# Moving z and the residual sum of x2 between ACT, GpSimd and DVE in an adaLN block with experts

## The chip, the cores and the metric

The kernel runs on one core of a Trainium2 chip. TensorE is called PE here, VectorE DVE, ScalarE ACT, GpSimd POOL and SyncE SP. The metric is the time of one execution on the device in microseconds; times are medians of several runs.

## The reference, cut to what matters

There are 16 batch elements of 512 tokens with 128 channels. For each one the block does attention and then a mixture of experts:

```python
h = layernorm(x) * (1 + ca) + sa
Q, K, V = (h @ W.T).reshape(16 heads, ...)            # 8 channels a head
out = softmax(Q @ K.T) @ V                            # in fp32 accuracy
y = out + h
x = x + ga * (y - mean(y)) / sqrt(var(y) + eps)       # mean and var over all 512 x 128 of the element
h = layernorm(x) * (1 + cb) + sb
logits = h @ gate_w;  top 2 of 8 experts, softmax weights
x = x + gb * weighted sum of the two experts' (silu(h @ w1 + b1) * (h @ w2 + b2)) @ w3 + b3
```

The code calls `z` the value ga * (y - mean) / sqrt(var + eps), with channels on partitions, and `x2` the sum x + z with tokens on partitions. x2 is the input of the second layernorm and, at the end, the residual of the output.

## The kernel before, in words

The attention part is a software pipeline of stages b = 0 to 16, one for each batch element and one more. A stage is 16 quads (r = 0 to 15) of four steps (h = 0 to 3). In step (b, r, h) PE makes a 128 x 512 tile of scores of element b (`pass_a`), DVE takes the negated row maximum of it from PSUM (`maximum`), and, 12 quads later, PE makes the tile again transposed with the maxima subtracted (`pass_b`), ACT takes its exponential (`exps`), and PE multiplies with V (`values`). Three PSUM banks hold the tiles of each pass, so PE is at most three tiles ahead of DVE and of ACT.

Everything else is put into the gaps of this stream, in an order written out by hand for each engine: `side(b, r, h)` on DVE, `stage` on POOL and SP, `before` and `halfway` on ACT, `misc_uses` on PE. Each engine works through its own list in order. One PSUM bank, `misc`, serves all small matmuls and transposes; the next fill of it waits until the one before has been read (`s_misc_read`). Stage b also finishes element b - 2 (its attention output, y, mean, variance, z, x2) and does the second layernorm, the routing and the row scatter of element b - 3.

The names which the steps speak of, in the order of a stage:

- z of element b - 2: ACT's `end_z` in quad 14 (L1822, an activation with scale and bias, which POOL's `y_move` computes as `y_scale` and `y_shift`, L918 and L920), PE's `z_turn` in quad 15, and DVE's `end_x2` (L1376), which reads the turned z in PSUM and adds x (`x_back`), after the last maximum of the stage.
- At the head of the next stage DVE does `front_x2` (`bn_stats` of x2, two tiles in step (0, 0) and two in (0, 2)), `front_sums` (L1253) in (1, 0), `end_inv` (L1299) in (2, 0) and `front_norm2` (L1390) in quad 3.
- POOL at the same time does `split_max` of the stage just ended (it needs all 64 maxima of it), `relay_v` (L900), `f_sums` and `front_power` (L911, L1030: 1/sqrt of the variance), `max_move` (L892, two DMAs), `scatter(b - 4, 1)` (four indirect DMAs, L1099), `front_rows` (L1037, L1044), `add_h` (L1018, L1025: y), `split_q`, `split_k`, `split_max` of the first half, `choose` and what follows it, `y_power`, `y_move`, `x_rows` (L991, L994), `places` (L973, which waits for DVE's `front_pos` in step (13, 3)), `second_score` (L968, which waits for DVE's `first_score` in (14, 1)), `front_slots`, and `scatter(b - 3, 0)`, four indirect DMAs more.
- PE turns `rows` in quad 5 (`h_turn`, L2046), needs `max_rows` in quads 1 and 9, and fills `v` in quad 0.
- ACT copies the normalized rows to the second slot (`row_copy`, L1839) in quad 12.
- After stage 16 an expert phase of 39 blocks follows, into which the last two elements' steps are woven. For these two, x2 is still made on DVE.

SP stores x2 (`x2_store`) and loads the next x (`x_back_load`) at the head of a stage, ahead of the store of `inv` and the loads of the next Q and K.

Of the kernel before, what the change touches and what calls it, by code (L numbers as in the profile page):

```python
# [125 lines left out]
def build(nc, x, wqT, wkT, wvT, w1, b1T, w2, b2T, w3, b3, gate_w, cT, wmod, out):  # L126
    ctx = ExitStack()
    with ctx:
# [255 lines left out]
        s_y_shift = sem("s_y_shift")  # L384
        s_z = sem("s_z")
        s_x2_stored = sem("s_x2_stored")

# [96 lines left out]
        def scattered(eng, n):  # L484

            eng.wait_ge(s_y_scattered[n % Y_RING], (n // Y_RING + 1) * BT * DMA)

        def wait_apart(eng, semaphore, value):
# [21 lines left out]
        def _(sp):  # L510
# [113 lines left out]
            def x_back_load(b):  # L624
                if later(b):
                    wait_apart(sp, s_misc_read, misc_index("z_turn", b - 1) + 1)
                sp.dma_start(x_back[:], x[b].rearrange("(t p) c -> p t c", p=P)).then_inc(s_x_back, DMA)

            def x2_store(b):
                wait_apart(sp, s_misc_read, misc_index("z_turn", b) + 1)  # L630
                sp.dma_start(x2_dram[b].rearrange("(t p) c -> p t c", p=P), x2_out[:]).then_inc(s_x2_stored, DMA)
# [202 lines left out]
        def _(pool):  # L834
# [52 lines left out]
            def max_move(b, side):  # L887

                pool.wait_ge(s_misc_read, misc_index("max_rows", b, side) + 1)
                for a in range(2):  # L890
# [3 lines left out]
                                   max_rows[at:at + PARTS * MCOLS // 2]).then_inc(s_max_moved, DMA)  # L894

            def relay_v(b, par):
                wait_apart(pool, s_v_loaded, (b + 1) * 4 * DMA)
                if later(b, 2):
                    wait_apart(pool, s_pv, (b - 1) * QUADS)
                pool.tensor_copy(Vt[:, par, :, 0:DK], v_land[:]).then_inc(s_v_relaid, 1)  # L900
# [11 lines left out]

            def y_move(b):

# [4 lines left out]
                pool.wait_ge(s_y_scale, b + 1)  # L919
                pool.tensor_tensor(y_shift[:], y_mean[:], y_scale[:], ALU.mult).then_inc(s_y_shift, 1)  # L920

# [160 lines left out]
            def front_slots(f):  # L1082
# [9 lines left out]
                pool.wait_ge(s_w_col, f + 1)  # L1092
                pool.wait_ge(s_h_row, 2 * (f + 1))
                pool.wait_ge(s_token, 2 * (f + 1))

            def scatter(f, k):

                for t in range(TT):
                    pool.indirect_dma_start(rows_dram, bass.IndirectOffsetOnAxis(ap=slot[:, k, t:t + 1], axis=0),  # L1099
                                            rows[:, f % 2, k, t], None).then_inc(s_scattered[f % 2], DMA)  # L1100

            def stage(b, par):
                if has(b, 1, NB):
                    split_max(b - 1, 1)
                if has(b, 0, NB - 1):
                    relay_v(b, par)
                if has(b, 3, NB):
                    f_sums(b - 3)
                    front_power(b - 3)
                if has(b, 1, NB):  # L1110
                    max_move(b - 1, 1)
                if has(b, 4, NB):
# [36 lines left out]
                if has(b, 2, NB - 1):  # L1149
                    y_move(b - 2)  # L1150
                if has(b, 1, NB - 4):
# [51 lines left out]
        def _(dve):  # L1203
# [175 lines left out]
            def front_x2(f, tiles):  # L1379

                dve.wait_ge(s_misc_read, misc_index("z_turn", f) + 1)
                for t in tiles:
# [204 lines left out]
            def side(b, r, h):  # L1587

                if has(b, 3, NB):
                    if r == 0 and h in (0, 2):  # L1590
                        front_x2(b - 3, (h, h + 1))
                    if (r, h) == (1, 0):
                        front_sums(b - 3)
                    if r == 3:
# [7 lines left out]
                if has(b, 2, NB + 1):  # L1602
                    if (r, h) == (2, 0):
                        end_inv(b - 2)
                    if (r, h) == (7, 0) and b == NB:
                        end_stats(b - 2)
# [55 lines left out]
            def stage(b, par):  # L1662
                for r in range(QUADS):
                    for h in range(4):
                        side(b, r, h)
                        if has(b, 0, NB - 1):
                            maximum(b, r, h)
                    if r == 15 and has(b, 2, NB - 1):
                        end_x2(b - 2)

# [101 lines left out]
        def _(act):  # L1772
            act.wait_ge(s_c, DMA)
            act.activation(c_silu[:], c_sb[:], ACT.Silu).then_inc(s_c_silu, 1)
            def evacuate(what, b, g=0):
# [24 lines left out]
                if what == "h_turn":  # L1800
                    if later(b):
                        act.wait_ge(s_misc_full, misc_index("logits", b - 1) + 1)
                    ins = act.activation(h2T[:], misc[:], ACT.Copy)
                ins.then_inc(s_misc_read, 1)

# [11 lines left out]
            def end_z(b):  # L1817

                act.wait_ge(s_y_shift, b + 1 if b < NB - 1 else NB - 1)
                if later(b):  # L1820
                    act.wait_ge(s_misc_full, misc_index("z_turn", b - 1) + 1)
                act.activation(z[:], y[:], ACT.Identity, bias=y_shift[:], scale=y_scale[:]).then_inc(s_z, 1)  # L1822
# [62 lines left out]
            def stage(b, par):  # L1885

                def before(r):
                    if r == 13 and has(b, 1, WCOPY):
                        expert_first(b - 1)
                    if r == 14 and has(b, 2, NB - 1):  # L1890
                        end_z(b - 2)
                    if r == 10 and has(b, 3, NB):
                        front_gap(b - 3)

                def halfway(r):
                    for q, what, ub, g in misc_uses(b):
                        if q == r and what in ("x_turn", "q", "k", "v", "max_rows", "h_turn"):
                            evacuate(what, ub, g)
                    if r == 7 and has(b, 2, NB - 1):
                        y_sum_all(b - 2)  # L1900
                    if r == 10 and has(b, 2, NB - 1):
                        y_squares(b - 2)
                    if r == 12 and has(b, 3, NB):
                        row_copy(b - 3)
# [331 lines left out]
```

## Time and profile before

| | us |
|---|---|
| median of 3 runs | 1076.61 (1074.5 to 1076.93) |
| the profiled execution | 1079.33 |
| its span, first to last instruction | 1077.6 |
| PE, DVE, ACT, POOL busy | 948.9, 899.9, 815.1, 725.5 |

The profile shows one execution. Busy time is the time in which an engine's instructions ran; issuing instructions and waits are not in it. A line of the timeline has the start and the length in microseconds, the engine, the line of the kernel, the operation with its output and inputs, and how many instructions were merged; in brackets stands the idle time ahead of it with the engine and line that ended it. The mean granted clock of PE over the span is 0.966 of its full speed.

### The profile page before, as it was taken

The page shows a single profiled execution, that of the slowest core. Times are in us where ns is not written, and L with a number is a line of the kernel's source. Part 1 is how long each engine was busy: PE and PEld are TensorE (multiplying, and loading weights), DVE is VectorE, ACT ScalarE, POOL GpSimd, SP SyncE. Part 2 cuts the span into 40 slices and gives each one's busy share as a digit, 9 for nine tenths or more (in the row PEclk, how much of TensorE's full clock was granted, in tenths as well). Part 3 has the DMA queues.
Part 4 walks back from the last instruction along what each step waited for, and adds up shares of the span by engine and source line. Part 5 has one row for each costly group of instructions (what it writes and reads, how often), then busy time and mean ns, then how long its engine had stood idle before and what let it go on. Part 6 is the DMA issues. An engine that isn't in the chain of part 4 may idle for free. (4 is left out here: it accounts for less than half of the span.)

```text
span 1077.6 us, 19369 instructions
## 1 busy us (share of the span) xinstructions
PE 948.9 (88%) x5725; PEld 362.9 (34%) x5725; DVE 899.9 (84%) x1891; ACT 815.1 (76%) x1563; POOL 725.5 (67%) x1198
## 2 busy tenths in 40 slices
PE   4699898999999999999999999889798998799970
PEld 2112122222222222222222222222135775577640
DVE  5797999998999999999999999999646767355766
ACT  2127898998889998999989999889676786477630
POOL 4853143877878778787787876665747677777761
PEclk9998999999999999999999999999799999899995
DMA  9859768756668567675676756631334445354546
GB/s 217 138 140 226 140 190 158 150 153 119 180 130 160 143 128 184 130 156 153 124 184 129 160 139 127 165 85 49 90 109 103 149 150 164 118 153 156 174 157 248
DMA packets 367832, 159.68 MB, mean 148 GB/s; under 512 B 289248, under 2 KB 332144, under 8 KB 364016
## 3 DMA queue, kind: packets, MB, share of 16 engines
q1 hardware_dynamic: 347376, 122.06, 50.7%
q0 software_dynamic: 11136, 19.61, 5.5%
q10 hardware_dynamic: 9216, 16.78, 4.5%
q8 instruction: 46, 0.75, 0.3%
q14 instruction: 58, 0.48, 0.2%
HBM read 87.85 MB, written 71.82 MB: 148 GB/s over the span
## 5 line engine op out<-in xcount | busy, mean ns | idle before, releaser
L1292 DVE TENSOR_REDUCE neg_max<-bank 128x1 f32<-128x512 f32 x1024 | 641.5, 681 | 40.5 <-PE bank L2071 35.2
L1848 ACT ACTIVATE probs<-bank 128x512 f32<-128x512 f32 x1024 | 545.7, 610 | 71.4 <-PE bank L2083 69.1
L2071 PE MATMUL bank<-Kt,Qt 48*128 48x512 bf16 x1024 | 336.6, 398 | 41.6 <-DVE neg_max L1292 31.8
L2083 PE MATMUL bank<-Qt,Kt 51*128 51x512 bf16 x1024 | 331.1, 392 | 7.9 <-ACT probs L1848 5.7
L2096 PE MATMUL bank<-probs,Vt 128*16 128x512 f32 x2048 | 275.4, 610 | 0.0
L2071 PEld LDWEIGHTS bank<-Kt,Qt 48*128 48x128 bf16 x1024 | 73.4, 94 | 374.0 <-DVE neg_max L1292 328.1
L1183 POOL DMA_INDIRECT y_dram<-y_rows,row_in x156 | 153.0, 981 | 58.3 <-issue 44.2
L1099 POOL DMA_INDIRECT rows_dram<-rows,slot x128 | 129.3, 1010 | 49.4 <-issue 35.2
L1974 ACT ACTIVATE probs<-bank,w3b_cur 128x512 f32<-128x512 f32 x78 | 53.5, 688 | 57.4 <-PE bank L2121 57.4
L1726 DVE SCALAR_TENSOR_TENSOR probs<-bank,w3b_cur,probs 128x512 f32<-128x512 f32 x78 | 58.3, 749 | 38.9 <-ACT probs L1974 38.2
L2083 PEld LDWEIGHTS bank<-Qt,Kt 51*128 51x128 bf16 x1024 | 74.5, 94 | 42.1 <-ACT probs L1848 34.1
L2187 PE MATMUL bank<-probs,w3b_cur 128*128 128x512 f32 x156 | 73.3, 592 | 0.0
L2119 PE MATMUL bank<-ht_first,w_cur 128*128 128x512 f32 x156 | 69.7, 447 | 1.7 <-DVE probs L1726 1.6
L1659 DVE TENSOR_TENSOR ht_rest<-bank,ht_first 128x512 fp32r<-128x512 f32 x39 | 26.9, 690 | 47.9 <-ACT ht_first L1946 47.7
L2120 PE MATMUL bank<-ht_rest,w_cur 128*128 128x512 f32 x156 | 62.7, 402 | 0.0
L2121 PE MATMUL bank<-ht_first,w_cur 128*128 128x512 f32 x156 | 62.2, 399 | 0.0
L2096 PEld LDWEIGHTS bank<-probs,Vt 128*16 128x16 f32 x2048 | 33.7, 94 | 74.5 <-issue 50.2
L892 POOL DMA_DIRECT2D Qt<-max_rows x64 | 43.9, 687 | 16.8 <-ACT max_rows L1799 15.0
L495 POOL CAST max_parts<-neg_max 128x32 bf16<-128x32 f32 x32 | 8.5, 265 | 55.6 <-DVE neg_max L1292 55.5
L1857 ACT ACTIVATE o_sb<-bank 128x512 f32<-128x512 f32 x64 | 38.5, 602 | 8.6 <-PE bank L2096 8.4
L1957 ACT ACTIVATE w_cur<-w_parts 128x1024 fp32r x37 | 39.1, 1057 | 0.2
L2106 PE MATMUL bank<-ident,row_in 128*128 128x128 f32 x156 | 24.4, 280 | 15.1 <-DMA row_in<-rows_dram 14.9
(254 smaller groups left out, 1237.6 us busy)
## 6 DMA issues: line engine op xcount, KB each, us to landing
o_dram<-o_sb ACTq DMA_DIRECT2D x64, 256.0 KB, 2.7
row_in<-rows_dram SPq DMA_DIRECT2D x39, 260.0 KB, 2.9
Qt<-q_dram SPq DMA_DIRECT2D x64, 128.0 KB
Kt<-k_dram SPq DMA_DIRECT2D x64, 128.0 KB
y_in<-y_dram SPq DMA_DIRECT2D x16, 512.0 KB, 4.6
q_dram<-q_parts SPq DMA_DIRECT2D x48, 128.0 KB, 4.9
k_dram<-k_parts SPq DMA_DIRECT2D x48, 128.0 KB, 5.8
rows_dram<-rows SPq DMA_DIRECT2D x4, 1040.0 KB, 5.3
```

Source lines behind the costliest of these rows:

```text
L1099: pool.indirect_dma_start(rows_dram, bass.IndirectOffsetOnAxis(ap=slot[:, k, t:t + 1], axis=0), rows[:, f % 2, k, t], None).then_inc(s_sca ...
L1183: pool.indirect_dma_start(y2_dram, bass.IndirectOffsetOnAxis(ap=row_in[n % RING][:, t, AT_TOKEN:AT_TOKEN + 1].bitcast(U32), axis=0), y_row ...
L1292: dve.tensor_reduce(neg_max[:, side, a, col:col + 1], score_a[m % 3][:], AX_X, ALU.max, negate=True).then_inc(s_max, 1)
L1726: dve.scalar_tensor_tensor(hidden[n % 2][:, c], up_value[c][:], w3b_cur[n % 3][:, AT_B2 + c:AT_B2 + c + 1], gate_act[c], ALU.add, ALU.mult ...
L1848: act.activation(probs[:, 4 * (j % 2) + (k ^ 1)], score_b[n % 3][:], ACT.Exp).then_inc(s_exp, 1)
L2071: pe.matmul(score_a[m % 3][:], Qt[b % BUFS][first:first + ROWS, n, P * c:P * c + P], Kt[b % BUFS][first:first + ROWS, n], start=True, stop ...
L2083: pe.matmul(score_b[m % 3][:], Kt[b % BUFS][first:first + ROWS + PARTS, n, P * c:P * c + P], Qt[b % BUFS][first:first + ROWS + PARTS, n], ...
L2096: ins = pe.matmul(pv_bank[32 * h:32 * h + 2 * DK, :], Vt[:, par, 4 * (N8 * a + n) + c], probs[:, 4 * (j % 2) + h], start=(c == 0), stop=(c ...
L2119: pe.matmul(to[:], w[:, 0, at], ht_first[n % 2][:], start=True, stop=False)
L2120: pe.matmul(to[:], w[:, 0, at], ht_rest[n % 2][:], start=False, stop=False)
L2121: ins = pe.matmul(to[:], w[:, 1, at], ht_first[n % 2][:], start=False, stop=True)
L2187: ins = pe.matmul(yt_bank[:], w3b_cur[n % 3][:, D * c:D * c + D], hidden[n % 2][:, c], start=(c == 0), stop=(c == HC - 1))
```

## The change

z of elements 0 to 13 is made on POOL by a `tensor_scalar` (`y_center` in place of `y_move`), which adds the negated mean and multiplies by the scale; `end_z` on ACT remains for the last element only. The turned z is copied from PSUM into `x2_out` by ACT, halfway through quad 15, in place of the sum on DVE; POOL adds x in place at the head of the next stage (`x2_add`), behind `split_max` and ahead of `relay_v`, and signals the new semaphore `s_x2`. The readers of x2 (`front_x2`, the store, the next load of x) wait for that. On POOL `max_move` now stands ahead of `f_sums` and `front_power`. On DVE `front_x2` goes from quad 0 to quad 1 and `front_sums` from (1, 0) to (2, 0), behind `end_inv`. `row_copy` goes from quad 12 to quad 15 on ACT, and the scatter of slot 0 no longer waits for it; that of slot 1 does.

```diff
+        def x2_made(eng, b):
+
+            if b < FIRST_LAST:
+                eng.wait_ge(s_x2, b + 1)
+            else:
+                eng.wait_ge(s_misc_read, misc_index("z_turn", b) + 1)
...
             def x_back_load(b):
                 if later(b):
-                    wait_apart(sp, s_misc_read, misc_index("z_turn", b - 1) + 1)
+                    x2_made(sp, b - 1)
...
             def x2_store(b):
-                wait_apart(sp, s_misc_read, misc_index("z_turn", b) + 1)
+                x2_made(sp, b)
...
+            def x2_add(b):
+
+                pool.wait_ge(s_misc_read, misc_index("z_turn", b) + 1)
+                pool.wait_ge(s_x_back, (b + 1) * DMA)
+                pool.tensor_tensor(x2_out[:], x2_out[:], x_back[:], ALU.add).then_inc(s_x2, 1)
...
-            def y_move(b):
+            def y_center(b):
...
-                pool.tensor_tensor(y_shift[:], y_mean[:], y_scale[:], ALU.mult).then_inc(s_y_shift, 1)
+                if b:
+                    pool.wait_ge(s_misc_full, misc_index("z_turn", b - 1) + 1)
+                pool.tensor_scalar(z[:], y[:], y_mean[:], y_scale[:], ALU.add, ALU.mult).then_inc(s_z, 1)
...
-                pool.wait_ge(s_h_row, 2 * (f + 1))
+                pool.wait_ge(s_h_row, 2 * f + 1)
...
             def scatter(f, k):
 
+                if k == 1:
+                    pool.wait_ge(s_h_row, 2 * (f + 1))
...
             def stage(b, par):
                 if has(b, 1, NB):
                     split_max(b - 1, 1)
+                if has(b, 3, NB):
+                    x2_add(b - 3)
                 if has(b, 0, NB - 1):
                     relay_v(b, par)
+                if has(b, 1, NB):
+                    max_move(b - 1, 1)
                 if has(b, 3, NB):
                     f_sums(b - 3)
                     front_power(b - 3)
-                if has(b, 1, NB):
-                    max_move(b - 1, 1)
...
                 if has(b, 2, NB - 1):
-                    y_move(b - 2)
+                    y_center(b - 2)
...
             def front_x2(f, tiles):
 
-                dve.wait_ge(s_misc_read, misc_index("z_turn", f) + 1)
+                x2_made(dve, f)
...
             def side(b, r, h):
 
                 if has(b, 3, NB):
-                    if r == 0 and h in (0, 2):
+                    if r == 1 and h in (0, 2):
                         front_x2(b - 3, (h, h + 1))
-                    if (r, h) == (1, 0):
-                        front_sums(b - 3)
...
+                if (r, h) == (2, 0) and has(b, 3, NB):
+                    front_sums(b - 3)
...
-                    if r == 15 and has(b, 2, NB - 1):
-                        end_x2(b - 2)
...
+                if what == "z_turn":
+                    if later(b):
+                        act.wait_ge(s_x2_stored, b * DMA)
+                        act.wait_ge(s_f_norm, TT * b)
+                    ins = act.activation(x2_out[:].rearrange("p t c -> p (t c)"), misc[:], ACT.Copy)
...
-                    if r == 14 and has(b, 2, NB - 1):
-                        end_z(b - 2)
...
+                    if r == 15 and has(b, 2, NB - 1):
+                        evacuate("z_turn", b - 2)
...
-                    if r == 12 and has(b, 3, NB):
+                    if r == 15 and has(b, 3, NB):
                         row_copy(b - 3)
```

## Rows read from the trace of the kernel before

**Rows 1.** The costliest group of instructions of the page.

```profile
L1292 DVE TENSOR_REDUCE neg_max<-bank 128x1 f32<-128x512 f32 x1024 | 641.5, 681 | 40.5 <-PE bank L2071 35.2
```

**Rows 2.** Windows: length; PE, PEld, DVE, ACT, POOL busy; clock, DMA. Stages 4, 9, 13.

```profile
228.30:274.90 46.60, 43.95 (x301) 12.60 (x299) 43.26 (x89) 41.62 (x84) 35.66 (x68) 0.96 0.65 143
453.45:498.10 44.65, 42.39 (x301) 12.56 (x299) 43.20 (x89) 40.50 (x83) 35.64 (x67) 1.00 0.68 152
632.30:677.00 44.70, 42.57 (x301) 12.59 (x299) 43.25 (x89) 40.55 (x83) 33.61 (x65) 1.00 0.66 144
```

**Rows 3.** Timeline of DVE around the head of stage 9.

```profile
445.21 4.44 DVE L1292 TENSOR_REDUCE neg_max<-bank 128x1 f32<-128x512 f32 x7
449.56 0.68 DVE L1376 TENSOR_TENSOR x_out<-bank,x_back 128x512 f32<-128x512 f32 x1
450.28 0.49 DVE L1383 BATCH_NORM_STATS2 f_stats<-x_out 128x6 f32<-128x128 f32 x2
450.68 1.27 DVE L1292 TENSOR_REDUCE neg_max<-bank 128x1 f32<-128x512 f32 x2
...
453.45 0.37 DVE L1253 BATCH_NORM_AGGREGATE f_mv<-f_stats 128x2 f32<-128x6 f32 x4
...
456.11 0.54 DVE L1299 RECIPROCAL inv<-den 128x64 f32<-128x64 f32 x1
456.56 2.42 DVE L1292 TENSOR_REDUCE neg_max<-bank 128x1 f32<-128x512 f32 x4
```

**Rows 4.** Timeline of POOL, from quad 11 of stage 8 to quad 4 of stage 9.

```profile
439.46 0.19 POOL L920 TENSOR_TENSOR y_shift<-y_mean,y_scale 128x1 f32<-128x1 f32 x1
...
443.63 0.32 POOL L973 TENSOR_TENSOR placed<-pick,pos 128x64 f32<-128x64 f32 x1 [1.81 <-DVE pos L1477]
...
445.37 0.20 POOL L968 TENSOR_TENSOR score<-gap_exp,score 128x4 f32<-128x4 f32 x1 [0.52 <-DVE score L1484]
...
450.70 0.96 POOL L1099 DMA_INDIRECT rows_dram<-rows,slot  x1 [0.30 <-issue]
451.66 0.22 POOL L495 CAST max_parts<-neg_max 128x32 bf16<-128x32 f32 x1
...
452.75 0.61 POOL L900 COPY Vt<-v_land 128x512 f32<-128x512 f32 x1
453.92 0.24 POOL L911 TENSOR_SCALAR f_ve<-f_mv 128x4 f32<-128x4 f32 x1 [0.56 <-DVE f_mv L1253]
...
456.97 1.09 POOL L1099 DMA_INDIRECT rows_dram<-rows,slot  x1 [0.30 <-issue]
...
461.22 0.96 POOL L1099 DMA_INDIRECT rows_dram<-rows,slot  x1 [0.30 <-issue]
...
463.56 1.29 POOL L1044 TENSOR_TENSOR rows<-f_scaled,mod_all 128x512 f32<-128x512 f32 x1
```

**Rows 5.** Timeline of PE in quad 5 of stage 9.

```profile
465.33 0.65 PE L2046 MATMUL bank<-ident,rows 128*128 128x128 f32 x4
```

**Rows 6.** Groups of instructions by line.

```profile
L1025 POOL TENSOR_TENSOR y<-attn,h_back 128x512 f32<-128x512 f32 x16 | 20.4, 1277 | 1.3
L1822 ACT ACTIVATE z<-y,y_shift,y_scale 128x512 f32<-128x512 f32 x15 | 13.1, 876 | 0.0
L1787 ACT ACTIVATE q_f<-bank 128x512 f32<-128x512 f32 x16 | 9.6, 597 | 8.8 <-PE bank L2024 7.5
L1011 POOL TENSOR_SCALAR z<-y,y_mean,y_scale 128x512 f32<-128x512 f32 x1 | 2.1, 2091 | 0.1
```

**Rows 7.** The head of stage 16: timelines of POOL, DVE and PE, and one stretch of the windows.

```profile
766.57 1.83 POOL L495 CAST max_parts<-neg_max 128x32 bf16<-128x32 f32 x1
...
766.11 2.23 DVE L1675 TENSOR_TENSOR w_parts<-w_parts 128x2048 fp32r<-128x2048 f32 x1
...
769.47 0.31 PE L2031 MATMUL bank<-ident_bf,max_parts 128*96 128x128 bf16 x1 [5.33 <-POOL max_parts L501]
...
772.00:784.00 12.00, 11.68 (x47) 2.57 (x44) 7.43 (x19) 6.84 (x14) 9.53 (x12) 0.50 0.09 26
```

More of the change, by code:

```diff
@@ L385, in build @@
         s_z = sem("s_z")
+        s_x2 = sem("s_x2")
         s_x2_stored = sem("s_x2_stored")
@@ L1604, in side @@
                         end_inv(b - 2)
+                if (r, h) == (2, 0) and has(b, 3, NB):
+                    front_sums(b - 3)
+                if has(b, 2, NB + 1):
                     if (r, h) == (7, 0) and b == NB:
@@ L1817, in end_z @@
             def end_z(b):
-                act.wait_ge(s_y_shift, b + 1 if b < NB - 1 else NB - 1)
-                if later(b):
-                    act.wait_ge(s_misc_full, misc_index("z_turn", b - 1) + 1)
+                act.wait_ge(s_y_shift, 1)
+                act.wait_ge(s_misc_full, misc_index("z_turn", b - 1) + 1)
                 act.activation(z[:], y[:], ACT.Identity, bias=y_shift[:], scale=y_scale[:]).then_inc(s_z, 1)
```

## The prediction

> **What bounds the kernel now.** I read the share of each engine by stage first, then one stage of the timeline of DVE, then the same stage on POOL, and last the place where the last attention stage differs. The costliest group is the row maximum on DVE, 1024 reductions of 681 ns [rows 1]. In a steady stage of 44.65 us DVE is busy 43.20 us, PE 42.39, ACT 40.50 and POOL 35.64 [rows 2]. That table makes DVE the bound and gives POOL about 9 us to spare. The timelines say more. On DVE nearly every instruction starts where the one before ends; `end_x2` starts at 449.56 and the next one at 450.28, so it holds DVE for 0.72 us [rows 3]. On POOL the reader should look not at the share but at where it really waits for another engine: 1.81 us for `pos`, 0.52 us for `score`, 0.56 us for `f_mv` [rows 4]. Less about 0.07 us of handover each, that is 1.74 + 0.45 + 0.49 = 2.7 us in a stage. The rest of the 9 us are gaps between scatter issues and short dependent steps, and they don't absorb anything. And POOL reaches the stage's head late: the last of its four scatters ends at 450.70 + 0.96 = 451.66, and only then does `split_max` start, 2.0 us after DVE's last maximum at 445.21 + 4.44 = 449.65 [rows 3, 4]. DVE doesn't feel that today, since nothing it does in the first two quads waits for POOL.
>
> **The change, part by part.**
>
> *DVE loses `end_x2`*: 0.72 us in each of the 14 stages 2 to 15, 10.1 us in all, the most this can give. The four `bn_stats` of x2 (0.40 us a pair: 450.28 to 450.68 is one) move from quad 0 to quad 1 and `front_sums` from quad 1 to quad 2, at the same cost.
>
> *ACT* loses `end_z` (876 ns) and gains a copy from PSUM like that of q (597 ns) [rows 6]: 0.3 us less a stage, on an engine with 4 us to spare. The row copy moves from quad 12 to quad 15, where it now stands beside the new copy. I take nothing for either: PE may not fill `v` until the z copy is read, but its quad 0 already needs exponentials that ACT makes after that copy, and any loss there falls ahead of the longer wait found below.
>
> *POOL gains z*: a `tensor_scalar` of 2091 ns (the one measured) for `y_shift` of 190 ns, +1.90 us [rows 4, 6]. Alone it would be hidden: it takes the place of the 1.74 us that POOL waits for `pos`, and PE turns z only in quad 15, after `pos`.
>
> *POOL gains `x2_add`*: no row shows it; the nearest, the add of y with the same shape and all operands in SBUF, takes 1277 ns [rows 6], which with the handover is 1.35 us. The multiply with a broadcast operand takes less, so 1.0 to 1.3 us; I take the row of the same form. It stands behind `split_max` and ahead of `relay_v`, and DVE now waits for it at quad 1.
>
> *When is x2 ready?* POOL's path from DVE's score: score 445.37 to the end of the scatters 451.66 is 6.29 us, `split_max` to 452.80 (`relay_v` starts at 452.75) is 1.14, `x2_add` 1.35: ready at 454.15 [rows 4]. DVE without `end_x2` ends the four maxima of quad 0 at 449.65 + 4 x 0.62 = 452.1 [rows 3]. It waits 2.0 us, against 0.72 saved. Behind it on DVE is queued the next stage's stream of maxima, on which PE's scores, and so everything, depend. That the scatter of slot 0 no longer waits for the row copy gives nothing: today's copy in quad 12 is over before `score` in quad 14, on which the scatters wait in any case.
>
> *The loop.* The wait also delays POOL, so I count a stage from one x2 (time X) to the next. From X, DVE needs 3.17 us for two pairs of `bn_stats` and four maxima (450.28 to 453.45), 0.45 for the reciprocal of `den`, 0.37 for `f_mv`, 0.17 for two handovers: `f_ve` at X + 4.2 [rows 3]. POOL has only `relay_v` and `max_move` for that time, 2.1 us, so it idles 2.0 us; before it idled 0.56. `f_ve` and the power take 1.36 us, four scatters 5.2 (456.97 to 462.18; the last starts at 461.22), `f_scaled` and `rows` 2.65: the rows stand at X + 13.4 (before: 464.85) [rows 4]. From there to the end of the next scatters the trace has 31.7 us, of which 1.74 + 0.45 are waits: 29.5 of work, plus 1.90 for z, 31.4. Then 1.14 + 1.35. The loop: 13.4 + 31.4 + 2.5 = 47.3 us against 44.65, **+2.6 us a stage**.
>
> *Cross-check through DVE.* From the start of `f_mv` to `score` on POOL it is 445.37 + 44.65 - 453.45 = 36.6 us [rows 2 to 4]. Add 0.86 for the `bn_stats` now inside, and 1.0 for PE: its `h_turn` came at 465.33 [rows 5], 11.9 us after `f_mv`, so it would come at X + 12.7 and finds rows only at X + 13.5. So 38.4 to the score, + 6.29 + 2.49 = 47.2. Both ways meet; neither engine has slack left to give to the other.
>
> *The sum.* At the head of stage 3 no scatters stand before `split_max`, so x2 is ready as DVE gets there (1.14 + 1.35 = 2.49 against 4 x 0.62 = 2.48): -0.6; the head of stage 4 is the first late one, 2.0 - 0.72 = +1.3. The eight stages 5 to 12 cost 2.6 each, 20.8. Stages 4, 13 and 14, where ACT copies weights or POOL loses `x_rows` and then the splits, are bound through `score`, which POOL's relief doesn't move: +2.5 each, 7.5. That is +29. The last stage gives some back. Today POOL's last scatter and first cast stand beside two DVE subtractions of about 2.2 us, the cast takes 1.83 us and PE waits 5.33 us for `split_max`; PE then runs at a granted clock of 0.50, its lower level of 1.2 GHz [rows 7]. With the DVE held back by x2, the subtractions fall behind `split_max`; PE gets `max_rows` some 4 us earlier, but the rows of that stage still wait for X + 13.4 or 2 us more. I take -2. In sum **+27 us**: 1079.3 + 27 = 1106.3 for the profiled execution, which stood 2.7 us above the median of 1076.6, so **1104 us** as the median.
>
> *A rule of the skill.* In the rows above, a cast that stands beside a two-operand SBUF subtraction on DVE is about seven times as long as its like in the middle stages (0.22 us at 451.66) [rows 4, 7]. The Trainium skill, "GPSIMD Engine Reference", section "Key points", says why it may be: POOL shares its SBUF interfaces with VectorE and contends with DVE instructions in a 2-port mode or with two SBUF inputs. By that rule 1.28 and 2.09 us hold in the steady stages, where DVE reads PSUM, and in the last stage the two subtractions move onto `max_move`, `f_ve` and the power. The sum by it would be 1106, by the row alone 1104.
>
> **The rivals.**
>
> *The cover holds* (faster). If POOL were at x2 when DVE reaches quad 1, DVE would keep its 0.72 us: 14 x 0.72 = 10.1, 1066.5 us. It decides at 452.1 against 454.15. Against it stands the start of `split_max` at 451.66, right behind the last scatter; for it only that spans on POOL are rough, by more than 2 us if it is to win. Chance 0.13.
>
> *Late, but no loop* (slower, less). If the time that DVE stands also relieves POOL, or the gaps between scatters shrink, only 2.0 - 0.72 = 1.3 us a stage is lost: 13 x 1.3 = 17, 1093 us. Chance 0.17.
>
> *The clock joins in* (slower, more). PE stands up to 2.4 us at each stage's head. In stage 4 the mean granted clock is 0.96 and the stage is 46.60 us, 1.95 longer than the steady one [rows 2]; part of that is a weight copy on ACT, so 1.95 is the upper bound and 0 the lower, and 1.5 us of it would hide behind the wait for rows. At 1.7 us in 12 stages +20: 1124 us. Chance 0.15.
>
> *It cancels* (no change). Quad 0 on PE, with `v`, is late by itself, the lateness costs DVE only as much as it saved, and POOL still has its gaps: 1077 us. Chance 0.05.
>
> **How the numbers follow.** The loop as worked out has a chance of 0.50: 1104 us. The unknown prices move it by 13 x 0.3 = 4 us each way, the last stage by 3. The range of 80% must take in the neighbours at 1093 and 1124: 1084 to 1126, which leaves out the cancelling case and the faster one. A measurement of this kernel can tell 0.3% (3 us) from no change. Faster 0.13, same 0.05, slower 0.82.
>
> **What would show it.** In the profile after: (1) the first `bn_stats` of a stage after an idle of 2 to 3.5 us on DVE put down to POOL's add; (2) no more wait of POOL for `pos`, and about 2 us for `f_mv`; (3) stages of 47.3 us, DVE's busy time in them 42.5; (4) PE's `h_turn` waiting for `rows`; (5) z at 2.09 and the add at 1.28 us; (6) `max_rows` of the last stage without its 5.33 us. I am wrong if the add starts before DVE has finished quad 0, if POOL's scatters turn out not to hold it, or if stages stay at 44.

## The result and the profile after

The change makes the kernel slower: 1104.99 us (median of 4 executions, 1097.31 to 1110.6) against 1076.77 (4 executions, 1074.5 to 1077.34), a ratio of 1.026 (1.023 to 1.029). The forecast was 1104. The profiled execution took 1097.31 us; the one of before took 1079.33. Medians and ranges here and below are over all executions of a kernel; the ratios leave out those more than 1.5% above its fastest one, which are one of 23 executions of the kernel before and three of 12 of z with the row copy, both on the third chip, and none elsewhere.

First the windows, one steady stage from `f_mv` to `f_mv` (columns as in [rows 2]), and under it a stretch in the last attention stage:

```profile
418.30:464.94 46.64, 41.94 (x295) 11.48 (x294) 42.85 (x87) 39.90 (x81) 37.53 (x68) 0.98 0.68 143
788.60:804.00 15.40, 12.91 (x51) 2.49 (x44) 13.37 (x38) 8.15 (x16) 11.49 (x13) 0.50 0.33 103
```

A stage of 44.65 us has become one of 46.64 [rows 2]. POOL's busy time grew by nearly as much, 1.9 us (35.64 to 37.53), but POOL stands free for 9.0 us of the stage before and 9.1 after, so its share doesn't say why the stage is longer; DVE lost 0.35. What the stage waits for is seen in the timeline of DVE. This is the stretch that answers to [rows 3], and below it every wait of DVE until the next head:

```profile
452.44 4.27 DVE L1312 TENSOR_REDUCE neg_max<-bank 128x1 f32<-128x512 f32 x7
456.94 1.29 DVE L1312 TENSOR_REDUCE neg_max<-bank 128x1 f32<-128x512 f32 x2 [0.23 <-issue]
458.78 1.29 DVE L1312 TENSOR_REDUCE neg_max<-bank 128x1 f32<-128x512 f32 x2 [0.55 <-PE bank L2094]
461.31 0.49 DVE L1403 BATCH_NORM_STATS2 f_stats<-x_out 128x6 f32<-128x128 f32 x2 [1.25 <-POOL x_out L908]
...
464.94 0.31 DVE L1273 BATCH_NORM_AGGREGATE f_mv<-f_stats 128x2 f32<-128x6 f32 x4
...
466.83 1.29 DVE L1312 TENSOR_REDUCE neg_max<-bank 128x1 f32<-128x512 f32 x2 [0.40 <-PE bank L2094]
473.06 1.29 DVE L1312 TENSOR_REDUCE neg_max<-bank 128x1 f32<-128x512 f32 x2 [0.27 <-PE bank L2094]
474.58 2.48 DVE L1312 TENSOR_REDUCE neg_max<-bank 128x1 f32<-128x512 f32 x4 [0.24 <-PE bank L2094]
477.24 3.17 DVE L1312 TENSOR_REDUCE neg_max<-bank 128x1 f32<-128x512 f32 x5 [0.17 <-PE bank L2094]
481.24 0.69 DVE L1312 TENSOR_REDUCE neg_max<-bank 128x1 f32<-128x512 f32 x1 [0.24 <-PE bank L2094]
488.20 4.36 DVE L1312 TENSOR_REDUCE neg_max<-bank 128x1 f32<-128x512 f32 x7 [0.23 <-PE bank L2094]
```

The reader should see two things. `end_x2` with its 0.72 us is gone, and at the head of the stage DVE stands 1.25 us for POOL's add. And DVE stands longer for PE: 0.23 + 0.55 us in quad 0 (the 0.23 is put down to `issue` in this stage and to PE's scores in most others) and 0.40 + 0.27 + 0.24 + 0.17 + 0.24 + 0.23 = 1.55 us in the rest of the stage, where the same list of before has four waits, 0.23 + 0.16 + 0.24 + 0.37 = 1.00 us, the last of them this one:

```profile
444.51 0.69 DVE L1292 TENSOR_REDUCE neg_max<-bank 128x1 f32<-128x512 f32 x1 [0.37 <-PE bank L2071]
```

The sum closes: 1.25 + 0.78 + 1.55 - 1.00 - 0.72 = +1.9 of the 2.0 us.

The timeline of POOL that answers to [rows 4]:

```profile
447.18 0.77 POOL L936 TENSOR_SCALAR z<-y,y_mean,y_scale 128x512 f32<-128x512 f32 x1
...
451.19 0.32 POOL L989 TENSOR_TENSOR placed<-pick,pos 128x64 f32<-128x64 f32 x1 [1.05 <-DVE pos L1497]
...
452.60 0.20 POOL L984 TENSOR_TENSOR score<-gap_exp,score 128x4 f32<-128x4 f32 x1 [0.19 <-DVE score L1504]
...
457.94 0.96 POOL L1117 DMA_INDIRECT rows_dram<-rows,slot  x1 [0.30 <-issue]
458.91 0.22 POOL L503 CAST max_parts<-neg_max 128x32 bf16<-128x32 f32 x1
...
460.01 1.26 POOL L908 TENSOR_TENSOR x_out<-x_out,x_back 128x512 f32<-128x512 f32 x1
461.22 0.61 POOL L914 COPY Vt<-v_land 128x512 f32<-128x512 f32 x1
...
465.35 0.23 POOL L925 TENSOR_SCALAR f_ve<-f_mv 128x4 f32<-128x4 f32 x1 [1.98 <-DVE f_mv L1273]
...
473.28 1.28 POOL L1060 TENSOR_TENSOR rows<-f_scaled,mod_all 128x512 f32<-128x512 f32 x1
```

The add starts right behind the last scatter and the 1.1 us of `split_max`, as forecast, and costs 1.26 us. But z costs 0.77 us, not 2.09, and so POOL still waits 1.05 us for `pos`. From here on X is the end of the add, 461.27. Wherever POOL ends its scatters, the add follows, DVE follows the add, and POOL's `f_ve` follows DVE.

How POOL's lateness comes back to DVE is seen on PE, here in stage 8:

```profile
428.01 0.63 PE L2069 MATMUL bank<-ident,rows 128*128 128x128 f32 x4 [0.66 <-POOL rows L1060]
...
439.42 0.23 PE L2054 MATMUL bank<-ident_bf,max_parts 128*96 128x128 bf16 x1 [0.55 <-POOL max_parts L509]
```

The first is `h_turn` in quad 5. From stage 4 on it starts 0.14 to 0.15 us behind the end of `rows` in every stage, where before, up to stage 15, it started 0.3 to 0.8 us behind and never stood idle for it. The second is the fill for `max_rows` in quad 9, which needs POOL's `split_max` of the first half: PE stands 0.51 to 0.55 us for it in all ten stages 4 to 13, and before only once, for 0.19. That closes the loop: x2, `f_mv`, `f_ve`, POOL's list down to `rows` and `split_max`, PE, the scores and with them DVE's `pos` and `score`, the scatters, `split_max`, the add.

Where the 18 us of the two profiled executions arose is seen at DVE's `inv`, which stands in step (2, 0) of every stage in both kernels. The second column of measured values is from another execution of the same kernel, shown below as an experiment:

| stretch | forecast, us | this profile | second profile |
|---|---|---|---|
| start to stage 3 | -0.6 | -1.9 | -1.4 |
| stage 3 | +1.3 | +1.1 | +1.1 |
| stage 4 | +2.5 | +1.1 | +1.1 |
| stages 5 to 12 | +20.8 | +15.9 | +15.8 |
| stages 13, 14 | +5.0 | +4.2 | +4.2 |
| stage 15, and the last stage with the experts | -2 | +5.5 - 7.9 | +5.5 + 2.6 |
| sum | +27 | +18.0 | +28.9 |

Up to stage 15 the two executions agree within half a microsecond, +20.4 and +20.8. The rest of the difference between them is in one stage, the last. The first row says little of the change: at `inv` of stage 2, ahead of every step that moved, the profiles of the kernels told of here stand anywhere from 136.3 to 141.8 us (before: 140.7). Without it the loop cost 22.3 and 22.2 us.

### The profile page after: what moved, and what is told of

It is laid out like the page before. It is cut to its first block and busy times, and to the rows that moved or that the text cites. A ratio compares the mean times of both kernels' runs of the same rounds, so it can differ in the third digit from the quotient of the medians.

```text
span 1095.6 us, 19369 instructions
## 1 busy us (share of the span) xinstructions
PE 943.5 (86%) x5725; PEld 357.2 (33%) x5725; DVE 893.8 (82%) x1877; ACT 815.7 (74%) x1563; POOL 751.1 (69%) x1212
## 5 line engine op out<-in xcount | busy, mean ns | idle before, releaser
L1312 DVE TENSOR_REDUCE neg_max<-bank 128x1 f32<-128x512 f32 x1024 | 644.4, 682 | 50.7 <-PE bank L2094 45.7
L1117 POOL DMA_INDIRECT rows_dram<-rows,slot x128 | 128.6, 1005 | 47.3 <-issue 34.5
L2106 PEld LDWEIGHTS bank<-Qt,Kt 51*128 51x128 bf16 x1024 | 71.7, 94 | 40.6 <-ACT probs L1871 30.6
```

What stands on the lines that cost most here:

```text
L1312: dve.tensor_reduce(neg_max[:, side, a, col:col + 1], score_a[m % 3][:], AX_X, ALU.max, negate=True).then_inc(s_max, 1)
L2106: pe.matmul(score_b[m % 3][:], Kt[b % BUFS][first:first + ROWS + PARTS, n, P * c:P * c + P], Qt[b % BUFS][first:first + ROWS + PARTS, n], ...
```

## The experiments

Ratios are against the kernel before on the same chip in the same runs; up to the last three experiments that is one of two chips, on which it takes 1077.42 and 1077.78 us. Where there is one execution only, the reading is that of its stages, and not of its time. The first two edits are cut from the difference against the kernel before, the others against the change unless it is said. The experiments are told in the order of the questions.

### Which part costs: z and the row copy alone, and x2 alone

```diff
-                pool.tensor_tensor(y_shift[:], y_mean[:], y_scale[:], ALU.mult).then_inc(s_y_shift, 1)
+                pool.tensor_scalar(z[:], y[:], y_mean[:], y_scale[:], ALU.add, ALU.mult).then_inc(s_z, 1)
...
-                    if r == 14 and has(b, 2, NB - 1):
-                        end_z(b - 2)
...
-                    if r == 12 and has(b, 3, NB):
+                    if r == 15 and has(b, 3, NB):
                         row_copy(b - 3)
```

> One part alone: z on POOL and the row copy in quad 15 as in the changed kernel, but x2 summed on DVE after the last maximum, bn_stats in quad 0 and front_sums in quad 1 as before. My theory (the loss comes from x2 being late at DVE's quad 1): z takes 0.77 us on POOL and fits into the 1.74 us for which POOL waited for pos, so stages stay at 44.6 to 44.7 us, POOL still waits about 1.1 us for pos, and the time is that of before, 1074 to 1080 us. The rival (POOL is full, each us given to it costs a us): 0.6 us a stage, 1084 us.

Measured: 1072.25 us (1069.7 to 1075.99, 5 executions), ratio 0.9945 (0.992 to 0.997). This part is a small gain. A steady stage is 44.1 to 44.2 us:

```profile
452.00:496.20 44.20, 41.94 (x301) 12.40 (x299) 43.18 (x89) 40.02 (x82) 36.29 (x68) 1.00 0.72 152
```

I had taken it for nothing, and the time lies below the 1074 to 1080 us expected. The other half:

```diff
+                if has(b, 3, NB):
+                    x2_add(b - 3)
...
-                    if r == 0 and h in (0, 2):
+                    if r == 1 and h in (0, 2):
...
-                    if r == 15 and has(b, 2, NB - 1):
-                        end_x2(b - 2)
...
+                    if r == 15 and has(b, 2, NB - 1):
+                        evacuate("z_turn", b - 2)
```

> The other part alone: ACT copies the turned z and POOL adds x at the stage's head, DVE reads x2 in quad 1, but z stays on ACT in quad 14 and the row copy in quad 12. My theory: DVE still waits 1.2 us for the add, stages are 46.5 to 46.7 us, bound by score to scatters to split_max to add, and the time is that of the changed kernel, 1097 to 1110 us. The rival (the loss needs both parts, since POOL must be full): stages near 46.1 us and 1090 us or less.

Measured: 1114.67 us (1111.05 to 1116.98, 4 executions), ratio 1.033 (1.030 to 1.035). The stages 5 to 13 are 47.0 us, but for two of 48.3 (7 and 13). Both the stage and the time are a little above what was expected, 46.5 to 46.7 and 1097 to 1110 us. Its head of a stage, POOL and DVE:

```profile
462.94 0.96 POOL L1113 DMA_INDIRECT rows_dram<-rows,slot  x1 [0.31 <-issue]
463.91 0.22 POOL L503 CAST max_parts<-neg_max 128x32 bf16<-128x32 f32 x1
...
465.01 1.26 POOL L908 TENSOR_TENSOR x_out<-x_out,x_back 128x512 f32<-128x512 f32 x1
...
470.36 0.23 POOL L925 TENSOR_SCALAR f_ve<-f_mv 128x4 f32<-128x4 f32 x1 [2.08 <-DVE f_mv L1269]
```

```profile
466.31 0.49 DVE L1399 BATCH_NORM_STATS2 f_stats<-x_out 128x6 f32<-128x128 f32 x2 [1.34 <-POOL x_out L908]
```

The wait is there without z. So z has no part in the loss. x2 alone loses 2.35 us a stage. The rest, which gains 0.5 without x2, takes 0.35 of that back and leaves the 2.0 measured. The two of 48.3 us each hold 6.8 us at a granted clock of 0.50, the lower level of 1.2 GHz; the change itself has such stretches too (3.4 us, 463.2 to 466.6 for one), but its stages are 46.7 with and without them.

### The spread from one execution to the next

The unchanged text of the change was run again, without an edit.

> The changed kernel once more, since its four executions lie at 1097 and 1101 and at 1109 and 1111 us with mean granted clocks of 0.967, 0.964, 0.956 and 0.949. If the clock makes the difference, the executions again come with the longer time at the lower clock, and the added 10 us lie where the granted clock falls: at the stages' heads by my rival, or in the last attention stage and the expert phase.

Measured: 1103.86 us (1098.92 to 1113.06, 4 executions), ratio 1.024 (1.017 to 1.031). Its profile took 1108.17 us, 10.9 more than the first one. The window of its last stage, to set beside the one at the top of this part:

```profile
788.60:829.20 40.60, 36.85 (x142) 8.68 (x134) 21.72 (x62) 21.89 (x43) 19.95 (x33) 0.50 0.35 105
```

```profile
804.20 1.09 PE L2069 MATMUL bank<-ident,rows 128*128 128x128 f32 x4 [0.34 <-POOL rows L1060]
...
840.32 1.05 PE L2065 MATMUL bank<-ident,z 128*128 128x128 f32 x4
```

In the first profile these two stand at 803.83 and 830.57. Both executions come to `h_turn` at the same time; the one that keeps the granted clock at 0.50 for 41 us instead of 17 takes 9.4 us longer from there to `z_turn` (36.1 against 26.7 us). Neither form is the usual one. Of the eight executions of this text, four took 1097 to 1101 us at mean granted clocks of 0.964 to 0.970, and four took 1108 to 1113 us at 0.949 to 0.960; the two profiles are one of each sort. The median of 1104.99 falls into the gap between the sorts and is the time of neither. That the six executions without a trace differ in the same stage isn't shown. What decides between 17 and 41 us I haven't found. The kernel before had 20 us of it in its profile.

### What the multiply costs: z by a subtraction

```diff
-                pool.tensor_scalar(z[:], y[:], y_mean[:], y_scale[:], ALU.add, ALU.mult).then_inc(s_z, 1)
+                pool.tensor_scalar(z[:], y[:], y_mean[:], y_scale[:], ALU.subtract, ALU.mult).then_inc(s_z, 1)
```

> The changed kernel with the tensor_scalar of z on POOL as subtract and multiply in place of add and multiply (the mean's sign is then wrong, the work is the same). In the last stage the subtracting form took 2.09 us, in the middle stages the adding form 0.77. If the operation makes the price, z takes 2.09 us in every stage, POOL no longer waits for pos, and the stage comes to the 47.3 us that I had worked out from 2.09, some 6 us more in all. If what runs beside it makes the price, z stays at 0.77 and the stage at 46.7.

Measured: 1101.56 us in one execution.

```profile
448.77 2.08 POOL L936 TENSOR_SCALAR z<-y,y_mean,y_scale 128x512 f32<-128x512 f32 x1
...
453.00 0.32 POOL L989 TENSOR_TENSOR placed<-pick,pos 128x64 f32<-128x64 f32 x1
...
454.20 0.20 POOL L984 TENSOR_TENSOR score<-gap_exp,score 128x4 f32<-128x4 f32 x1
...
461.60 1.26 POOL L908 TENSOR_TENSOR x_out<-x_out,x_back 128x512 f32<-128x512 f32 x1
```

One word in the code makes z 2.08 us instead of 0.77. The row of before on which I had built [rows 6] is of the last element, whose z is written with the subtraction. The waits for `pos` and `score` vanish, as my working said they would with z at 2.09; but the stage stays at 46.7 us where the POOL path was to give 47.3. POOL's path with the dear z is thus as long as the path through PE and DVE, and not longer. z stands in POOL's list behind the `split_max` for which PE waits in quad 9 and ahead of `score`, and in between the loop runs through PE and DVE: there POOL had 1.05 + 0.19 us of waits to give.

### Is it the length of the add: one column of it

```diff
-                pool.tensor_tensor(x2_out[:], x2_out[:], x_back[:], ALU.add).then_inc(s_x2, 1)
+                pool.tensor_tensor(x2_out[:, 0, 0:1], x2_out[:, 0, 0:1], x_back[:, 0, 0:1], ALU.add).then_inc(s_x2, 1)
```

> The changed kernel, but POOL's add of x takes one column instead of 512, so the residual is left out of x2 but for one channel of one tile; all waits stay. My theory (the stage runs from DVE's score through the scatters, split_max and the add back to DVE): the add falls from 1.26 to about 0.2 us, DVE's wait for it from 1.22 to 0.2, and the stage from 46.7 to 45.6 us, still above the 44.65 of before. The rival (DVE's wait is a symptom, and PE or ACT in quads 15 and 0 hold the stage): the stage stays at 46.5 or more.

Measured: 1085.32 us in one execution.

```profile
415.30:460.90 45.60, 41.98 (x301) 12.04 (x300) 42.91 (x88) 40.50 (x83) 36.41 (x68) 1.00 0.68 147
```

```profile
457.04 0.19 POOL L908 TENSOR_TENSOR x_out<-x_out,x_back 128x1 f32<-128x1 f32 x1
```

```profile
457.26 0.49 DVE L1403 BATCH_NORM_STATS2 f_stats<-x_out 128x6 f32<-128x128 f32 x2 [0.16 <-POOL x_out L908]
```

The add is 1.07 us shorter and the stage 1.07 us shorter: microsecond for microsecond, the add lies on the path. And 45.6 is still 1.4 us above the 44.2 of z and the row copy alone: PE's waits in quads 5 and 9, 0.65 and 0.53 us, stay as they were, so the loop is still closed. So even an add that costs nothing would lose here: it is enough that x2 must pass through POOL's list behind the scatters.

### Readers a quad later

`front_x2`, `front_sums`, `front_norm2` and PE's `h_turn` each stand one quad later.

```diff
-        (1, "max_rows", b - 1, 1), (5, "h_turn", b - 3, 0), (7, "logits", b - 3, 0), (13, "pos", b - 3, 0), (8, "mean", b - 2, 0),
+        (1, "max_rows", b - 1, 1), (6 if b < NB else 5, "h_turn", b - 3, 0), (7, "logits", b - 3, 0), (13, "pos", b - 3, 0), (8, "mean", b - 2, 0),
...
-                    if r == 1 and h in (0, 2):
+                    if r == (2 if b < NB else 1) and h in (0, 2):
...
-                    if r == 3:
+                    if r == (4 if b < NB else 3):
...
-                if (r, h) == (2, 0) and has(b, 3, NB):
+                if (r, h) == (3 if b < NB else 2, 0) and has(b, 3, NB):
```

> The changed kernel with everything on DVE and PE that reads x2 one quad later in stages 3 to 15: bn_stats in quad 2, front_sums in quad 3, front_norm2 in quad 4, h_turn in quad 6. If only DVE's wait for the add counts, it is gone, since DVE arrives 2.5 us later than now, and the stage is 44 us or less. If POOL is full (my loop), POOL now waits 4.4 us for f_mv in place of 1.95, its list takes 45.4 + 2.5, and the stage grows to about 47.9 us.

Measured: 1122.89 us in one execution, stages of 48.0 to 50.0 us.

```profile
474.72 1.26 POOL L908 TENSOR_TENSOR x_out<-x_out,x_back 128x512 f32<-128x512 f32 x1
...
481.44 0.23 POOL L925 TENSOR_SCALAR f_ve<-f_mv 128x4 f32<-128x4 f32 x1 [3.34 <-DVE f_mv L1273]
```

```profile
453.78 1.29 DVE L1312 TENSOR_REDUCE neg_max<-bank 128x1 f32<-128x512 f32 x2 [2.49 <-PE bank L2094]
```

DVE waits no more for the add, and the kernel is slower still. The wait has moved to POOL, which stands 3.34 us for `f_mv` (1.98 before the edit, 4.4 expected), and what stands behind it comes later by as much. This speaks for the loop over POOL and against the view that DVE's wait is the whole loss. Most stages came out 1 to 2 us longer than expected. Where the time goes is in PE's timeline just ahead of DVE's wait of 2.49 us:

```profile
453.19 0.23 PE L2054 MATMUL bank<-ident_bf,max_parts 128*96 128x128 bf16 x1 [3.01 <-POOL max_parts L509]
```

The stream of scores stops in quad 9 for POOL's `split_max`, 3.0 us in each of the nine stages 4 to 12 (0.5 in the change), and in quad 5, now 6, another 1.05 us for `rows`.

### The scatters elsewhere in POOL's list

Slot 0 is scattered in the next stage between `max_move` and `f_sums`, and slot 1 ahead of `y_power`, so that no scatter stands between the second score and `split_max`. `front_norm2` and `h_turn` stand one quad later, as in the experiment above, and `front_rows` behind `add_h`.

```diff
+                if has(b, 4, NB):
+                    scatter(b - 4, 0)
                 if has(b, 3, NB):
                     f_sums(b - 3)
                     front_power(b - 3)
...
-                if has(b, 3, NB):
-                    front_rows(b - 3)
                 if has(b, 2, NB + 1):
                     add_h(b - 2)
+                if has(b, 3, NB):
+                    front_rows(b - 3)
...
+                if has(b, 4, NB - 1):
+                    scatter(b - 4, 1)
...
-                    scatter(b - 3, 0)
+                    if b == NB:
+                        scatter(b - 3, 0)
```

> The changed kernel with the scatters of slot 0 taken from the tail of POOL's stage to the head of the next, behind max_move, where POOL waits for f_mv; those of slot 1 behind gap_one; add_h ahead of front_rows; front_norm2 in quad 4 and h_turn in quad 6. By my theory split_max then starts with DVE's last maximum, the add is done when DVE has finished quad 0 (2.49 against 2.48 us), DVE no longer waits for POOL, and it keeps the 0.72 us of end_x2 and what ACT's relief gives: stages of 43.5 to 44.2 us, the whole 1060 to 1072 us. If the add is late for another reason, stages stay at 46.

Measured: 1110.18 us (1105.39 to 1121.13, 4 executions), ratio 1.032 (1.025 to 1.039). A miss: the stages are 46.2 us, not about 44.

```profile
460.37 1.27 POOL L908 TENSOR_TENSOR x_out<-x_out,x_back 128x512 f32<-128x512 f32 x1
464.12 1.39 POOL L900 DMA_DIRECT2D Qt<-max_rows  x2 [1.92 <-ACT max_rows L1823]
...
475.98 1.27 POOL L1053 TENSOR_TENSOR f_scaled<-f_norm,mod_all 128x512 f32<-128x512 f32 x1 [1.02 <-DVE f_norm L1415]
```

```profile
460.86 1.29 DVE L1317 TENSOR_REDUCE neg_max<-bank 128x1 f32<-128x512 f32 x2 [0.55 <-PE bank L2099]
...
472.22 0.75 DVE L1415 TENSOR_SCALAR f_norm<-x_out,f_mv,f_rstd 128x128 f32<-128x128 f32 x1 [0.97 <-POOL f_rstd L1046]
```

Up to stage 15 nothing waits for the add any more, so the scatters were what held it. But the time that POOL gained at the head it lost to new waits: 1.92 us for ACT's `max_rows`, 1.02 for `f_norm`, while DVE waits 0.97 for `f_rstd`, ahead of which four scatters now stand. DVE's own work grew too: two of its four `f_norm` take 0.75 and 0.70 us here, while POOL makes y, and 0.34 otherwise. Neither of these two edits found an order of the lists in which the add is free; others weren't tried.

### Where the gain of z and the row copy comes from

The kernel with z and the row copy alone, but the copy back in quad 12:

```diff
-                    if r == 15 and has(b, 3, NB):
+                    if r == 12 and has(b, 3, NB):
                         row_copy(b - 3)
```

> z alone on POOL, as in the run that was 5 us faster than before, but with the row copy back in quad 12. Its stages were 44.1 us against 44.65. If the gain is z's 0.88 us taken from ACT's quad 14, it stays: 44.1 to 44.2. If it is the row copy taken from quad 12, where ACT also copies o, the stage is back at 44.5 or more.

Measured: 1075.03 us in one execution; stages of 44.5 us.

```profile
442.79 0.69 DVE L1307 TENSOR_REDUCE neg_max<-bank 128x1 f32<-128x512 f32 x1 [0.37 <-PE bank L2089]
```

With the copy in quad 15 the stages are 44.15 and the wait of 0.37 us behind `pos` is not in DVE's timeline:

```profile
442.53 1.41 DVE L1307 TENSOR_REDUCE neg_max<-bank 128x1 f32<-128x512 f32 x2
```

The kernel before has the same 0.37 us. So of the 0.5 us a stage about 0.3 comes from moving the copy on ACT (44.47 to 44.15) and 0.2 from z (44.65 to 44.47), each by one pair of profiles.

The copy alone, against before, and the kernel with z and the copy once more, were run on a third chip, on which before takes 1140.71 us (1133.66 to 1151.17, 23 executions):

> The kernel before with one part of the change alone: the row copy on ACT in quad 15 in place of quad 12, with the scatter of slot 0 no longer waiting for it. With z on POOL the stage was 44.15 us with the copy in quad 15 and 44.5 with it in quad 12, before 44.65. If the gain is the copy's place by itself, the stage is 44.3 us and the whole 1071 to 1075 us. If it needs z off ACT's quad 14, since ACT is behind in quads 12 to 15 either way, the stage stays at 44.6 us and the whole at 1076 to 1079 us.

> z on POOL and the row copy in quad 15, x2 as before, once more with more rounds: stages of 44.1 to 44.2 us and 1070 to 1075 us, 0.3 to 0.8% under the kernel before. If its first five executions were lucky ones of the last stage's clock, it comes to within 0.3% of it.

Measured: 1137.08 us for the copy alone (10 executions), ratio 0.995 (0.992 to 0.998), and 1136.05 us for both (12 executions), ratio 0.9955 (0.992 to 0.999). The gain of half a per cent is there on this chip as well, and the copy alone has it too; between the two the intervals don't decide.

### The add ahead of split_max

```diff
-                if has(b, 1, NB):
-                    split_max(b - 1, 1)
                 if has(b, 3, NB):
                     x2_add(b - 3)
+                if has(b, 1, NB):
+                    split_max(b - 1, 1)
```

> The changed kernel with POOL's add of x ahead of split_max at the stage's head. By my theory the add then starts right behind the last scatter and DVE gets x2 1.14 us sooner: its wait of 1.22 us all but vanishes, and the stage falls from 46.7 to about 45.6 us. max_rows on PE then comes 1.3 us after x2 in place of 1.2 us ahead of it; if that is the wait that counts in turn, PE starves DVE in quad 1 and the stage stays near 46.5 us.

Measured: 1146.84 us in one execution on that third chip, stages of 46.2 to 48.3, mostly 47.3 us.

```profile
461.78 1.29 DVE L1312 TENSOR_REDUCE neg_max<-bank 128x1 f32<-128x512 f32 x2 [0.99 <-PE bank L2094]
464.00 1.29 DVE L1312 TENSOR_REDUCE neg_max<-bank 128x1 f32<-128x512 f32 x2 [0.93 <-PE bank L2094]
465.21 0.47 DVE L1403 BATCH_NORM_STATS2 f_stats<-x_out 128x6 f32<-128x128 f32 x2
```

DVE no longer waits for the add but stands 1.9 us for PE in quad 0. The stage can't be set against 46.7, since z and the copy alone have stages of 45.4 to 46.0 on this chip and 44.2 on the first. Against the 45.7 it is 1.6 us longer; the change is 2.5 longer on the first chip. That hints at a gain of some 0.9 us from the order, but it isn't a measurement, and the expected 45.6 is neither shown nor refuted.

## Why the prediction came out as it did

**The mechanism** was the one forecast. `split_max` starts where the last scatter ends (457.94 + 0.96 = 458.90), the add starts 1.1 us later (1.14 forecast), DVE waits for it; POOL then waits 1.98 us for `f_mv` (2.0 forecast). From DVE's last maximum of a stage to x2 it was to be 454.15 - 449.65 = 4.50 us and is 461.27 - 456.71 = 4.56. The wait of 2.0 us that I gave to the add is there as 1.25 for the add and 0.23 + 0.55 for PE ahead of it. From `score` to x2 it was to be 8.78 us and is 8.67. The add was sized by the row of y at 1.28 us [rows 6] and is 1.26. Of the signs named, three came out otherwise: POOL still waits for `pos`, z isn't at 2.09, and DVE's idle time put down to the add is 1.25 us and not 2 to 3.5. DVE's busy time in the stage is 42.85 us for the 42.5 named.

**The loop was 0.6 us too long**, 47.3 (47.2 by the cross-check) against 46.7. PE does wait for `rows`, as forecast. In the stage shown `h_turn` starts at 474.70, X + 13.4, 0.14 us behind the end of `rows` at 474.56; its row has no idle time, but its like in stage 8 has 0.66 us, and so have most. In the cross-check this term was put at 1.0 us, though its own X + 12.7 and X + 13.5 give 0.8. From X to the next `score` it is 499.28 - 461.27 = 38.0 us, and without the term the cross-check has 36.6 + 0.86 = 37.4. So the whole delay by PE, `rows` in quad 5 and `max_rows` in quad 9 together, is 0.6 for 1.0; the wait in quad 9 wasn't forecast. In the sum over POOL's list the failing term is z. That sum has a slip as well: from the rows at 464.85 to the end of the next scatters at 451.66 + 44.65 = 496.31 it is 31.5 us and not 31.7. With both set right the two ways give 47.1 and 47.0.

**z was mis-sized**: +1.90 us forecast, +0.58 measured (0.77 - 0.19). I took the one row with that name and shape [rows 6] and didn't look at its operation: subtract and multiply there, add and multiply in the diff. The diff and the line numbers showed this. It did not reach the stage, because the path through PE and DVE was as long; with the subtraction put back, the stage is the same 46.7. "Both ways meet" was right as a statement on 46.7 and wrong on 47.3, and that neither engine has slack to give holds only for the dear z. The 0.6 that POOL's path is shorter than my sum, with z at 2.08, is spread: 0.1 in X to `f_ve`, 0.1 in `split_max` and the add, 0.4 in the work between, of which 0.25 is the slip.

**ACT was not nothing.** "I take nothing for either" was wrong by 0.3 us a stage for the row copy, some 4 us in all, and ACT's relief from z gave 0.2 more. For the copy a rule of the argument was at fault: I looked at whether the copy hides in its new place and not at whom it disturbs in the old one. In quad 12 it takes 0.63 us of ACT, and DVE's wait of 0.37 us for PE behind `pos` was in the trace of before; that the one makes the other I read from the pair of runs with the copy in either place, not from a chain in the trace.

**The last stage** was sized at -2. Counted from stage 15 on it is -2.4 in the first profile and +8.1 in the second. `max_rows` came earlier, as forecast:

```profile
787.46 0.31 PE L2054 MATMUL bank<-ident_bf,max_parts 128*96 128x128 bf16 x1 [1.64 <-POOL max_parts L509]
```

with 1.64 us of wait for 5.33 [rows 7]. Not forecast was that DVE, with no maxima of a next stage to do, stands 5.67 us for the add there:

```profile
788.57 0.49 DVE L1403 BATCH_NORM_STATS2 f_stats<-x_out 128x6 f32<-128x128 f32 x2 [5.67 <-POOL x_out L908]
```

I had applied the wait of the steady head (2.0) to a head without a quad 0. And the length of the stretch at the lower clock, 17 or 41 us, was taken as that of before.

**So 1104 was hit by luck.** The stages ahead of 15 were to give +29 and gave +20.4 and +20.8, of which the loop's length explains 5 in stages 5 to 12 and stage 4 another 1.4 (it gave 1.1 for 2.5; why, I didn't work out). From stage 15 on it was -2.4 or +8.1 where I had -2. For the profiled execution I had 1106.3; the two profiled took 1097.3 and 1108.2, and the median met the forecast because it fell between the two sorts of execution. The range of 1084 to 1126 was meant for such things, but the central number is better than its working.

**The rule of the Trainium skill** ("GPSIMD Engine Reference", "Key points": POOL contends with DVE instructions that read two SBUF inputs) was said to move the slow spans onto `max_move`, `f_ve` and the power in the last stage. By that rule, the trace agrees for `f_ve`. Two rows, of POOL and of DVE:

```profile
792.43 2.17 POOL L925 TENSOR_SCALAR f_ve<-f_mv 128x4 f32<-128x4 f32 x1 [2.61 <-DVE f_mv L1273]
```

```profile
792.25 2.26 DVE L1694 TENSOR_TENSOR w_parts<-w_parts 128x2048 fp32r<-128x2048 f32 x1
```

`f_ve` takes 2.17 us beside the subtraction and 0.23 in the steady stages, and the cast that took 1.83 [rows 7], eight times the steady 0.22, now takes 0.22, with no subtraction beside it. `max_move` and the power kept their 1.33 and 1.06 us: of the two subtractions one stands beside `f_ve`, and the other, from 788.98 on, began while `max_move` was under way. The rows show that the two go together; no run removed the subtractions.

**The rivals.** *The cover holds*: no, the add is late in all 12 heads from stage 4 to 15, by 1.20 to 1.30 us in eleven of them and 1.88 in the last. *Late, but no loop* (1.3 us a stage): the measured 2.0 includes what z and the row copy give, and x2 alone costs 2.35; and in the experiment with readers a quad later DVE had no wait for the add and the stage grew, with PE standing for POOL. Both speak against it. *The clock joins in*: in the steady stages of the change it doesn't; two stages of x2 alone, with 6.8 us at the lower clock, are 1.3 us longer than the rest; in the last stage it goes with 9.4 of the 10.9 us between the two profiled executions. It came in where I hadn't put it. *It cancels*: no.

## What to carry to other kernels

An engine with a fifth of its time free can still be the last to arrive: before a step is moved to it, find at which moment of the stage its list reaches that step and who is next in need of the result; here an add of one column, 0.2 us, still lost 1.4 us a stage against the same kernel with x2 on DVE. Price a step by the row with the same operation, not only the same name and shape. And look at a moved step's old place as well as its new one: the row copy, moved for another reason, gave more than half of what this change gained, and with z on GpSimd but x2 left on DVE the kernel beats the one before by half a per cent.

## What was not expected of the hardware

- On POOL a `tensor_scalar` of 128x512 floats took 0.77 us with add and multiply and 2.08 us with subtract and multiply, in otherwise equal kernels.
- After a stall at the same place the granted clock stayed at 0.50 for 17 us in one profiled execution and for 41 us in the other of the same kernel; 9.4 of the 10.9 us between the two lie in this stretch.
- On POOL a 128x4 `tensor_scalar` of 0.23 us took 2.17 us beside one two-input DVE subtraction of 2.26 us, and ended 0.1 us behind it.
- The same kernel before took 1077.4 us on one chip and 1140.7 on another. On the second the attention stages of z and the copy alone were 1.5 us longer and its expert phase, from the last `f_mv` on, 253 us against 223. Why, the runs don't say.
